# Layer norms of a macaron block: the inverse deviation as one power on GpSimd in place of a square root on ScalarE and a reciprocal on VectorE

## What is computed

```
x = x + 0.5 * ffn(layernorm(x))        # gate, up, down: 4096 wide, 4-bit weights with block scales, tanh gelu
x = x + attention(layernorm(x))        # 16 heads of 32, causal
x = x + 0.5 * ffn(layernorm(x))
layernorm(x) = (x - mean(x)) / sqrt(var(x) + 1e-5)
```

## Time and profile before

| | before |
|---|---|
| median of 3 runs | 3096.09 us (3094.86 to 3097.19) |
| the profiled execution | 3098.18 us, span in the profile 3096.4 us |
| PE busy | 2950.7 us, 95% |
| DVE busy | 1852.0 us, 60% |
| ACT busy | 1062.8 us, 34% |
| POOL busy | 759.8 us, 25% |
| instructions on POOL | 481 |

### The profile page before, as it was taken

How to read it: one execution, slowest core, us unless ns; L and a number is a source line. 1 busy time by engine, 2 the same in 40 slices (tenths; PEclk the granted TensorE clock), 3 DMA queues, 4 the chain that set the end, 5 groups by cost and what they waited for, 6 DMA issues and landing times. The chain is left out here.

```text
span 3096.4 us, 38962 instructions
## 1 busy us (share of the span) xinstructions
PE 2950.7 (95%) x13152; PEld 2207.2 (71%) x13152; DVE 1852.0 (60%) x3290; ACT 1062.8 (34%) x1797; POOL 759.8 (25%) x481
## 2 busy tenths in 40 slices
PE   5999999999999979999999996689999999999999
PEld 3788888888888858644444443458888888888887
DVE  7666655665656564666666661476655666556554
ACT  4322222222222232355665554142222222222222
POOL 4322222222222245200000001343222222222221
PEclk8999999999999999999999998789999999999999
DMA  3000000000000027622222221201000000000001
GB/s 95 21 28 28 21 27 20 27 20 27 27 20 20 1 58 170 173 56 55 55 56 55 55 53 52 79 7 35 27 22 20 27 25 23 27 20 24 24 14 55
DMA packets 120569, 127.58 MB, mean 41 GB/s; under 512 B 72672, under 2 KB 72928, under 8 KB 117152
## 3 DMA queue, kind: packets, MB, share of 16 engines
q1 hardware_dynamic: 119928, 125.93, 15.6%
q10 hardware_dynamic: 552, 0.59, 0.1%
HBM read 96.87 MB, written 29.62 MB: 41 GB/s over the span
## 5 line engine op out<-in xcount | busy, mean ns | idle before, releaser
L61 PE MATMUL psum<-ffn_x_high,ffn_w_high 128*128 128x512 f32 x2048 | 804.5, 393 | 14.5 <-DVE ffn_gelu L389 14.5
L62 PE MATMUL psum<-ffn_x_low,ffn_w_high 128*128 128x512 f32 x2048 | 799.2, 390 | 0.0
L63 PE MATMUL psum<-ffn_x_high,ffn_w_low 128*128 128x512 f32 x2048 | 799.0, 390 | 0.0
L526 POOL TENSOR_TENSOR ffn_inner<-ffn_gelu,ffn_inner 128x512 fp32r<-128x512 f32 x256 | 346.3, 1353 | 1156.4 <-ACT ffn_inner L471 1156.4
L379 DVE SCALAR_TENSOR_TENSOR ffn_gelu<-ffn_gelu,psum 128x512 f32<-128x512 f32 x256 | 176.0, 688 | 599.1 <-ACT ffn_gelu L464 599.0
L61 PEld LDWEIGHTS psum<-ffn_x_high,ffn_w_high 128*128 128x128 f32 x2048 | 386.6, 189 | 99.3 <-DVE ffn_gelu L389 17.3
L62 PEld LDWEIGHTS psum<-ffn_x_low,ffn_w_high 128*128 128x128 f32 x2048 | 386.2, 189 | 82.4 <-issue 2.6
L63 PEld LDWEIGHTS psum<-ffn_x_high,ffn_w_low 128*128 128x128 f32 x2048 | 385.9, 188 | 80.7
L61 PE MATMUL psum<-ffn_inner,ffn_w_high 128*128 128x512 f32 x1024 | 398.6, 389 | 0.2
L62 PE MATMUL psum<-ffn_inner,ffn_w_high 128*128 128x512 f32 x1024 | 398.4, 389 | 0.0
L63 PE MATMUL psum<-ffn_inner,ffn_w_low 128*128 128x512 f32 x1024 | 398.4, 389 | 0.0
(11 more groups left out here) (114 smaller groups left out, 3056.9 us busy)
## 6 DMA issues: line engine op xcount, KB each, us to landing
ffn_words<-packed SPq DMA_DIRECT2D x96, 256.0 KB
ffn_word_scales<-scales SPq DMA_DIRECT2D x96, 256.0 KB
qk_parts<-parts SPq DMA_DIRECT2D x32, 512.0 KB, 4.1
queries<-qk_parts SPq DMA_DIRECT2D x48, 256.0 KB, 4.0
keys<-qk_parts SPq DMA_DIRECT2D x48, 256.0 KB, 6.2
x<-x_in SPq DMA_DIRECT2D x4, 1024.0 KB, 15.0
v_parts<-parts SPq DMA_DIRECT2D x16, 256.0 KB, 4.7
values<-v_parts SPq DMA_DIRECT2D x16, 256.0 KB, 7.6
```

The source lines that it names most:

```text
L61: pe.matmul(out, w_high, x_high, start=first, stop=False, skip_group_check=True)
L62: pe.matmul(out, w_high, x_low, start=False, stop=False, skip_group_check=True)
L63: return pe.matmul(out, w_low, x_high, start=False, stop=last, skip_group_check=True)
L526: pool.tensor_tensor(inner[:, tb % 2, m, 1, :], product[m], f32(inner[:, tb % 2, m, 0, :]), ALU.subtract)\
```

## The change

The square root on ACT becomes `Identity` with eps as bias: it only carries variance + eps out of PSUM, which POOL cannot read there. POOL then raises `std` in place to the power of -0.5, as a `tensor_tensor` of 128x512 whose second operand is a 128x1 tile of -0.5 read for every column. The reciprocal on DVE is gone. `rstd_ready` is now raised by POOL, and DVE's `scale` waits for it alone. The power stands on POOL's stream ahead of the `low` of the same block. One memset of 128x1 per norm is added on DVE.

```diff
+        self.power = ctx.enter_context(nc.sbuf_tensor(f"{tag}_power", [P, 1], F32))
...
-        act.activation(self.std[:], self.var_bank[tb % 2], ACT.Sqrt, bias=self.eps[:]).then_inc(self.std_ready, 1)
+        act.activation(self.std[:], self.var_bank[tb % 2], ACT.Identity, bias=self.eps[:]).then_inc(self.std_ready, 1)
+
+    def reciprocal_root(self, pool, tb):
+        if tb == 0:
+            pool.wait_ge(self.constants_ready, 3)
+        pool.wait_ge(self.std_ready, tb + 1)
+        pool.tensor_tensor(self.std[:], self.std[:], self.power[:].broadcast_to([P, TB]), ALU.pow).then_inc(self.rstd_ready, 1)
 
     def scale(self, dve, tb):
-        dve.wait_ge(self.std_ready, tb + 1)
-        dve.reciprocal(self.std[:], self.std[:]).then_inc(self.rstd_ready, 1)
         dve.wait_ge(self.rstd_ready, tb + 1)
...
             dve.memset(eps[:], EPS).then_inc(n.constants_ready, 1)
+            dve.memset(n.power[:], -0.5).then_inc(n.constants_ready, 1)
...
             weight_low(0, 0, UP)
+            n.reciprocal_root(pool, 0)
             n.low(pool, 0)
             n.sum_pairs(pool, 3)
+            n.reciprocal_root(pool, 1)
             n.low(pool, 1)
             gelu_tiles(0, 0, 0)
             weight_low(0, 0, DOWN)
+            n.reciprocal_root(pool, 2)
             n.low(pool, 2)
             gelu_tiles(0, 0, 1)
+            n.reciprocal_root(pool, 3)
             n.low(pool, 3)
```

## The result

| | before | after |
|---|---|---|
| median | 3096.45 us (3094.86 to 3097.19, 4 runs) | 4042.57 us (4041.45 to 4043.86, 4 runs) |
| ratio | | 1.3057, 95% interval 1.3042 to 1.3073 |
| span in the profile | 3096.4 us | 4041.0 us |
| PE busy | 2950.7 us, 95% | 2963.5 us, 73% |
| DVE busy | 1852.0 us | 1811.1 us |

A forecast was written before the change was run, and what follows sets the result against it. PE was taken as the bound, but in the norm stretches the chain of waits through the reciprocals. 12Z - 40.7 at Z = 9.4 gave +72, the clock +10: 3180 profiled, 3178 us against the median, range 3090 to 3310.

The forecast's parts named there:

- I take 9.4: POOL, all norms: one power takes 9.4 us, the middle between one and two iterated functions (6.3 and 12.6).
- the upper bound of 20.6: POOL, all norms: a power as two polynomials of some eight passes each, 16 plain operations of 1.29 us, takes 20.6.
- rival (c): All norms: the power is much dearer, 16 us or more; 3313 us at 20.6, 12 more per microsecond; chance 0.20.
- Z: The unknown time of one 128x512 power on POOL, twelve in all; put between 1.3 and 20.6 us.
- Second block: Both FFNs' norms: the power and DVE's unpack exclude each other, Z - 3.3; with the port free Z - 5.5.
- Third and fourth block: FFN norms: third Z - 1.6 behind weight_low, and -0.6 for the tanh's load; fourth Z - 3.3, less 1.2 swallowed.
- project_in: Its norm's four blocks: Z - 3.1, Z - 3.0, Z - 4.3 and Z - 5.0, slack included; sum 4Z - 15.4.
- The clock: PE after five new waits, three in project_in, one behind each FFN's fourth block: lower clock costs 5 x 2 = +10 us.
- (a): All norms: the power costs no more than a plain POOL operation, Z = 1.3; 3085 us, faster; chance 0.10.
- (b): All norms: the power is as fast as DVE's reciprocal, Z between 2.0 and 3.6; 3101 us, same; chance 0.08.
- the forecast's own case: All norms: Z from 3.6 to 16, slower; 3178 us at Z = 9.4; chance 0.62.
- (d): DVE and ACT: their saved time, 40 and 18 us, counts; the prediction said it does not and gave no separate chance.

The follow-up runs named there:

- e3: The changed kernel with a plain POOL multiplication by 1.0 instead of the power, std ready made by ACT's inverse square root: 3085.03 us, ratio 0.9963 against before.
- e1: The kernel before with nine powers and one multiplication on scratch tiles at the head of POOL's stream: 20.735 us for 128 columns, 1.006 for 4.
- e5: The kernel before with 150 DVE multiplications beside one POOL power, then 20 POOL multiplications, at its head: 225 ns each beside the power, 324 beside multiplications.
- e6: The kernel before with ACT's Identity in place of Sqrt and DVE's reciprocal kept, so 13 of 14 table loads go: 3093.49 us, ratio 0.9995.
- e9: The changed kernel with a power of only 16 columns into a scratch tile, std ready made by ACT's inverse square root: 3097.0 us, ratio 1.0001 against before.
- e2: The changed kernel with a power of only 64 columns into a scratch tile, std ready made by ACT's inverse square root: 3187.17 us, 1.029 times before.
- e4: The kernel before with ACT's Abs_reciprocal_sqrt in place of Sqrt, and no reciprocal or power anywhere: 3082.57 us, ratio 0.9949.
- e7: The kernel before with Ln and Exp on ACT in place of the square root, and no reciprocal: 3083.52 us, ratio 0.9962.

## Why the prediction was right in form and wrong in size

**The step that failed is "I take 9.4", and behind it the upper bound of 20.6.** It scaled DVE's reciprocal against a plain operation (4.9) to POOL, and then allowed two functions of eight passes, each at the price of a plain operation. The power measured 81.9, four times that bound and 71 to 79 times the 1.04 to 1.15 of the plain operation that e3 put in its place. Nothing in the trace of before stood for a power, and the scaling took a ratio measured on DVE for one on POOL. On POOL the ratio of a power to a multiplication of the same size is 52 in e1, where one iterated function was given 4.9 and the bound 16. The step that failed with it is the range: the text itself says of rival (c) "no row that limits it", prices it at 12 us for each microsecond, and then stops the range at 3310, since it took the bound of an assumed method for a bound of the cost. With the measured Z the formula gives 12 x 81.93 - 40.7 + 10 = 952; measured +944.6 in the span. Rival (c), which had 0.20, is what happened. Two ends in the prediction are also added up loosely: Z = 20 gives 3305 and not 3310, and Z = 4 gives 3103 without the clock's term and 3113 with it, not 3105. Neither bears on the miss.

Block by block, as `scale` starts. DVE's timeline after, in ffn1:

```profile
112.20 3.57 DVE L166 TENSOR_TENSOR ffn_centred<-ffn_centred,ffn_std 128x512 f32<-128x512 f32 x4 [84.41 <-POOL ffn_std L160]
...
123.85 1.15 DVE L369 TENSOR_SCALAR ffn_nibbles<-ffn_nibbles 128x512 int32<-128x512 int32 x1
125.03 1.22 DVE L375 TENSOR_TENSOR ffn_weight<-ffn_nibbles,ffn_word_scales 128x1024 f32<-128x1024 f16 x1
...
205.64 3.57 DVE L166 TENSOR_TENSOR ffn_centred<-ffn_centred,ffn_std 128x512 f32<-128x512 f32 x4 [79.39 <-POOL ffn_std L160]
...
307.90 3.57 DVE L166 TENSOR_TENSOR ffn_centred<-ffn_centred,ffn_std 128x512 f32<-128x512 f32 x4 [84.14 <-POOL ffn_std L160]
...
407.20 3.57 DVE L166 TENSOR_TENSOR ffn_centred<-ffn_centred,ffn_std 128x512 f32<-128x512 f32 x4 [81.84 <-POOL ffn_std L160]
```

and POOL's:

```profile
120.46 2.81 POOL L105 TENSOR_TENSOR ffn_pairs<-x 128x1024 f32<-128x1024 f32 x1
123.22 82.38 POOL L160 TENSOR_TENSOR ffn_std<-ffn_std,ffn_power 128x512 f32<-128x512 f32 x1
...
223.56 2.42 POOL L526 TENSOR_TENSOR ffn_w_low<-ffn_weight,ffn_w_high 128x1024 fp32r<-128x1024 f32 x1
225.93 81.93 POOL L160 TENSOR_TENSOR ffn_std<-ffn_std,ffn_power 128x512 f32<-128x512 f32 x1
```

The distance from one `scale` to the next, less the same distance before, gives each block's term:

| ffn1 | predicted | measured |
|---|---|---|
| first | Z - 2.1 | 112.20 - 32.78 = 79.42 = Z - 2.5 |
| second | Z - 3.3, or Z - 5.5 with the port free | 93.44 - 16.67 = 76.77 = Z - 5.2 |
| third | Z - 1.6 | 102.26 - 22.04 = 80.22 = Z - 1.7 |
| fourth, with the tanh's load | Z - 3.9 | 99.30 - 21.23 = 78.07 = Z - 3.9 |
| swallowed behind it, the clock counted apart | 1.2 | 1.4, the rest of +313.04 |

- *First block*: right. POOL's weight piece sets the start, and came 0.3 us sooner.
- *Second block*: wrong in its assumption. The two-operand L375 ran in its usual 1.22 beside the power; only the start was shared, 0.45 us on the power and 0.72 on L369. e5 shows the same apart from everything else. It was worth 2 x 2.2, the 4.4 us that the prediction had put beside it.
- *Third and fourth block*: right. The power starts as `weight_low` ends (223.56 + 2.42, then 225.93). Behind the fourth 1.4 is swallowed, near the 1.2 that was read from the two waits; the clock's 2 us do not show.
- *ffn2*: predicted 4Z - 13.2, with the port free 4Z - 15.4, and 2 us more for the clock; measured 4Z - 15.4, without those 2.
- *project_in*: predicted 4Z - 15.4 and 3 x 2 us for the clock, so 4Z - 9.4; measured 4Z - 9.5. That the sum fits to 0.1 is in part luck, since the parts don't. `scale` started at 1521.71, 1614.08, 1709.91 and 1802.28, in a stage that began at 1422.28; before, the same starts were 19.04 after the stage's begin and then 13.53, 15.45 and 12.92 apart. So the blocks came out as Z - 1.5, Z - 3.1, Z - 1.5 and Z - 2.5, and 0.8 was swallowed at the end. Predicted were Z - 3.1, Z - 3.0, Z - 4.3 and Z - 5.0, the slack included, with the clock counted apart. The 1.6 us of the first block come from a place that the prediction doesn't have: in the first 11 us of the stage the granted clock was 0.61, where it had been 1.00. The first two `mean` took 2.84 and 3.78 us and not 1.95 and 1.98, so `wv_low` ended 17.5 us after the stage's begin and not 15.8, and the power stands behind it. No run shows that the change does this: the traces of all the other kernels here, e5's and e6's with the reciprocal among them, have 0.60 to 0.84 in these 11 us, and only that of before has 1.00. The wait ahead of the first `mean` is the same in both. PE's timeline before, and after:

```profile
1110.70 1.95 PE L115 MATMUL psum<-qkv_pairs,qkv_averager 128*128 128x512 f32 x4 [2.57 <-DVE qkv_pairs L104]
1115.14 1.98 PE L115 MATMUL psum<-qkv_pairs,qkv_averager 128*128 128x512 f32 x4 [2.49 <-POOL qkv_pairs L104]
```
```profile
1423.75 2.84 PE L116 MATMUL psum<-qkv_pairs,qkv_averager 128*128 128x512 f32 x4 [2.57 <-DVE qkv_pairs L105]
1429.08 3.78 PE L116 MATMUL psum<-qkv_pairs,qkv_averager 128*128 128x512 f32 x4 [2.49 <-POOL qkv_pairs L105]
```

- *The clock*: +10 for five places. In project_in it is visible beyond the first 11 us, in PE's variance matmuls of the third and fourth block, 3.78 where the fourth had 1.88:

```profile
1623.38 3.78 PE L146 MATMUL psum<-qkv_squares,qkv_averager 128*128 128x512 f32 x4 [79.49 <-DVE qkv_squares L138]
...
1715.75 3.78 PE L146 MATMUL psum<-qkv_squares,qkv_averager 128*128 128x512 f32 x4 [76.29 <-DVE qkv_squares L138]
```

  PE had just waited 79.49 and 76.29 us; the stretch from 1614 to 1628 had a granted clock of 0.50. In ffn1 the clock's 2 us are not there, although the clock was 0.50 from 410 to 414, behind the fourth `scale`: the slack accounts for the stage without them, and so it does in ffn2. So some 4 of the 10 us were too many, and of the places in project_in one is the stage's begin, where the change adds no wait. PE's busy time rose by 12.8 us in the whole program, so "PE's busy time unchanged" was wrong by what the lower clock costs.
- *Table loads*: one is left, as predicted. e6 puts the worth of all of them between nothing and 4.3 us; the prediction had 1.2 for the two tanh loads in its sum, and e6's ffn1 shows 0.5 for the one there.
- *The rivals*: (a), (b) and the forecast's own case were each built, as e3, e9 and e2, and each came out within 10 us of the time the prediction gave it (3085, 3101 and, for its Z of 9.4, 3178). (d), that DVE's and ACT's saved time counts, is excluded by e4, which takes the same twelve reciprocals off DVE, 40 us, and gains 14, and by e6, which takes 14 loads off ACT, 18 us, and gains 4.3 at most.
- e4 shows a gap in the block terms themselves when the operation is short or gone. I had let a start that comes earlier be worth its full time; it is worth that only if POOL is not in a long subtraction just then.

## What to carry to other kernels

An operation for which the trace has no row should be timed alone, in one run of a few instructions, before a kernel is built around it; a bound from an assumed method is no bound, and with twelve of them on the chain each microsecond of error is twelve. Where all partitions hold the same value, look at what the engine's cost counts: here only columns do, and a power of 128x4, which holds as many values as one block has tokens, took 1 us in e1. What it would cost to bring the variances into that layout was not tried. And when a step is taken off the path, look at what it had kept apart: here the gain of removing the reciprocal went from 14 to 23 us once long subtractions of POOL were moved out of the way, though the same moves with the reciprocal in place gained nothing. Last, look at the clock in the one trace that all differences are taken from: in project_in the trace of before was the exception.

## What the runs showed of the hardware

- A power on GpSimd costs 159 ns for each column and 0.4 us fixed, whatever the number of partitions (1 to 128) and the exponent (-0.5, 0.5, 1, 2) (e1).
- It does not slow DVE's operations with two SBUF operands: 225 ns each beside it and 226 alone, against 324 beside POOL's multiplications (e5).
- A GpSimd multiplication of 128x512 by one value for each partition took 1.04 us in project_in and 1.15 in the FFNs (e3), where the subtraction of two full tiles took 1.29.
- ACT's Abs_reciprocal_sqrt takes the 0.69 us of the square root and replaces root, reciprocal and power (e4).
- Ln and Exp one behind the other had a load of 1.28 us between them each time (e7), and the second function began 0.02 us behind the load.
- PE's granted clock at the begin of project_in, behind a matmul stretch at 1.00 and a wait of 2.6 us, was 0.60 to 1.00 over 11 us in thirteen traces of nearly the same instructions there.
